# A pairwise-similarity stage: node blocks 15 and 16 away computed from both sides, and fourteen instead of fifteen column blocks added per span

## The reference

```
A = (dist == 1) + eye(N)
nrm = maximum(sqrt(sum(X * X, axis=1)), EPS)
sim = X @ X.T / (nrm[:, None] * nrm[None, :])
m = (A + sim) * 0.5
d = exp(diagonal(m) - logsumexp(m, axis=1))
out = relu(X * d[:, None])
```

## Time and profile before

| | |
|---|---|
| median of three runs | 365.58 us |
| profiled execution, its own time | 365.37 us |
| its span, first to last instruction | 363.6 us |
| mean granted TensorE clock | 0.892 |
| VectorE busy | 302.0 us (83%) |
| TensorE matmul busy | 283.4 us (78%) |
| ScalarE busy | 160.1 us (44%) |
| VectorE's adds, L1099 | 73.0 us in 64 instructions |
| span matmuls, L1394 | 64.7 us in 256 |
| span exponentials, L752 | 60.1 us in 32 |

### The profile page before, as it was taken

The page is one execution under the profiler, slowest core; times in us unless marked ns, Lnnn a source line. Parts: engine busy times, 40 slices in busy tenths (PEclk is TensorE's granted clock), DMA queues, the critical chain, the costliest instruction groups (busy, mean ns, idle before and its releaser), DMA issues.

```text
span 363.6 us, 5779 instructions
## 1 busy us (share of the span) xinstructions
PE 283.4 (78%) x2126; PEld 167.0 (46%) x2126; DVE 302.0 (83%) x422; ACT 160.1 (44%) x251; POOL 102.2 (28%) x107
## 2 busy tenths in 40 slices
PE   7598886118979984599999978758989999965094
PEld 7246754108554431256667623755333333344051
DVE  3899998898367789998688965684999999998764
ACT  1599522200424966500000000397988888994000
POOL 3011069850000098792850005001850000000000
PEclk9899989556999996599999998669999999998569
DMA  3410000000000000000000000344000000000713
GB/s 122 139 46 2 7 6 1 0 0 3 0 2 0 0 0 0 2 0 2 2 2 2 2 1 0 126 107 144 7 0 0 0 0 0 0 3 0 173 58 115
DMA packets 12697, 9.73 MB, mean 27 GB/s; under 512 B 7426, under 2 KB 11010, under 8 KB 12674
## 3 DMA queue, kind: packets, MB, share of 16 engines
q1 hardware_dynamic: 10866, 7.72, 7.4%
q10 hardware_dynamic: 1808, 1.70, 1.6%
HBM read 5.23 MB, written 3.15 MB: 23 GB/s over the span
## 4 chain that ended last, share of the span: by engine, by line
PE 48%; DVE 24%; issue 17%; ACT 4%; ACTq 2%; DMA 2%; DVEq 1%
PE ps L1281 13%; PE ps L1165 11%; PE ps L1178 7%; PE ps L1295 5%; DVE arena L1099 3%; PE ps L1374 2%; PE ps L1197 2%; PE ps L1394 2%; PE ps L1439 2%; DVE arena L365 2%; DVE arena L1015 2%; ACT arena L752 1%; ACTq L344 1%; PE ps L1190 1%; DVE arena L355 1%
## 5 line engine op out<-in xcount | busy, mean ns | idle before, releaser
L1099 DVE TENSOR_TENSOR arena<-arena 128x1024 f32 x64 | 73.0, 1224 | 4.4 <-ACT arena L752 4.4
L1394 PE MATMUL ps<-arena 128*128 (+1 forms) x256 | 64.7, 380 | 6.2 <-ACT arena L752 5.0
L752 ACT ACTIVATE arena<-ps 128x2048 f32<-128x2048 f32 x32 | 60.1, 1877 | 8.5 <-PE ps L1394 6.9
L600 ACT ACTIVATE rstd<-mv,eps 128x2 f32<-128x2 f32 (+1 forms) x5 | 1.5, 296 | 97.5 <-DVE mv L813 97.5
L1394 PEld LDWEIGHTS ps<-arena 128*128 (+1 forms) x256 | 24.4, 97 | 42.1 <-issue 15.8
L1281 PE MATMUL ps<-turns,shift 64*64 64x512 f32 x200 | 36.6, 623 | 4.2 <-DVE turns L1041 4.2
L1165 PE MATMUL ps<-turns,k 128*128 128x512 f32 x80 | 36.5, 618 | 4.2 <-DVE turns L1051 2.1
L1295 PE MATMUL ps<-arena,shift 64*64 64x256 f32 x192 | 34.6, 399 | 6.1 <-DVE arena L1015 6.1
L1041 DVE TENSOR_TENSOR turns<-arena,ps 128x1024 f32<-128x1024 f32 x30 | 35.4, 1216 | 2.4 <-PE ps L1295 2.2
L556 POOL TENSOR_TENSOR arena<-arena 128x2304 f32<-128x2304 f32 x6 | 31.6, 5268 | 16.2 <-PE ps L1295 12.7
L1178 PE MATMUL ps<-arena 64*64 64x240 f32 (+3 forms) x576 | 31.3, 373 | 1.7 <-DVE arena L355 1.7
(11 more groups left out here) (227 smaller groups left out, 503.3 us busy)
## 6 DMA issues: line engine op xcount, KB each, us to landing
scratch_x<-xs SPq DMA_DIRECT2D x4, 256.0 KB
arena<-arena SPq DMA_DIRECT2D x2, 512.0 KB, 3.5
scratch_x<-arena SPq DMA_DIRECT2D x2, 512.0 KB, 3.5
arena<-scratch_x ACTq DMA_DIRECT2D x2, 512.0 KB, 3.7
out<-arena SPq DMA_DIRECT2D x4, 256.0 KB, 2.1
sN<-in_bias_n SPq DMA_DIRECT2D x48, 0.0 KB
xs<-in_x SPq DMA_DIRECT2D x8, 64.0 KB
xs<-in_x ACTq DMA_DIRECT2D x8, 64.0 KB
```

The lines of the kernel that those rows point to most:

```text
L752: act.activation(E[k], ps[:, (k % 2) * 2048:(k % 2 + 1) * 2048], ACT.Exp, scale=0.5 / SPLIT ** 2, accum_out=rowsum[:, bass.ds(i, 1)]).then ...
L1099: dve.tensor_tensor(out=cc, in0=cc, in1=E[k][:, lo * P:hi * P], op=ALU.add).then_inc(sem(name), 1)
L1394: ins = pe.matmul(bank(b0 + q), w, m[:, bass.ds(i * P + 512 * q, 512)], start=(t == 0), stop=(t == 1 and q > 0))
```

## The change

The span is computed as before, 16 blocks wide, row sums included, but only blocks 1 to 14 are added to `colacc`; the far add is 7 blocks (896 columns) instead of 8 (1024). Blocks 15 away therefore lack their mirror image, which is block 17 away of the other row block. The far stage computes it: it has for each row block the blocks 16 and 17 away, 256 columns, in four stages of eight row blocks (`FAR` gives PSUM side and first row block). Stages 1, 2 and 3 all use side 1. On TensorE stages 0 to 2 are issued behind the loop, then the transposes of half 1, then stage 3, then the transposes of half 0. The waits are renumbered: stages 0 and 1 wait for `exp_done` 31 and 32, stage 2 for 34, stage 3 for 35.

```
+        FAR = ((0, 16), (1, 24), (1, 0), (1, 8))
 ScalarE
-            for t in range(2):
+            for t, (side, first) in enumerate(FAR):
                 act.wait_ge(sem("col_near"), NODE_BLOCKS - 2 + t)
                 act.wait_ge(sem("far_done"), t + 1)
-                for i in range(REACH):
-                    c, row = i * P, REACH * (1 - t) + i
-                    ins = act.activation(E[t][:, c:c + P], ps[:, t * 2048 + c:t * 2048 + c + P], ACT.Exp,
+                for i in range(8):
+                    c, row = i * 2 * P, first + i
+                    ins = act.activation(E[t][:, c:c + 2 * P], ps[:, side * 2048 + c:side * 2048 + c + 2 * P], ACT.Exp,
                                          scale=0.5 / SPLIT ** 2, accum_out=row16[:, row:row + 1])
 VectorE
-                for name, lo, hi in (("col_far", 8, REACH), ("col_near", 1, 8)):
+                for name, lo, hi in (("col_far", 8, REACH - 1), ("col_near", 1, 8)):
...
-                dve.wait_ge(sem("exp_done"), NODE_BLOCKS + 2 - h)
+                dve.wait_ge(sem("exp_done"), NODE_BLOCKS + 4 - 2 * h)
 TensorE
-            for t in range(2):
-                pe.wait_ge(sem("exp_done"), NODE_BLOCKS - 1 + t)
-                for i in range(REACH):
-                    ins = half_products(view(ps, t * 2048 + i * P, [(1, P)]), i + REACH * (1 - t), (i + REACH * t) * P, P)
+            def far(t):
+                side, first = FAR[t]
+                pe.wait_ge(sem("exp_done"), NODE_BLOCKS - 1 + t if t < 2 else NODE_BLOCKS + t)
+                for i in range(8):
+                    ins = half_products(view(ps, side * 2048 + i * 2 * P, [(1, 2 * P)]), first + i,
+                                        ((first + i + REACH) % NODE_BLOCKS) * P, 2 * P)
                 ins.then_inc(sem("far_done"), 1)
+
+            for t in range(3):
+                far(t)
             pe.wait_ge(sem("col_far"), NODE_BLOCKS + 1)
             pe.wait_ge(sem("col_near"), NODE_BLOCKS + 1)
             for h in (1, 0):
-                pe.wait_ge(sem("exp_done"), NODE_BLOCKS + 2 - h)
                 if h == 0:
+                    far(3)
                     pe.wait_ge(sem("col_folded"), 1)
+                    pe.wait_ge(sem("exp_done"), NODE_BLOCKS + 4)
```

## The result

The changed kernel takes 369.52 us (median of four runs) against 365.79 us for before: a ratio of 1.0087, 95% interval 1.0056 to 1.0119. Run again beside the experiments it gave 369.95 against 365.57 us, ratio 1.0123 (1.0091 to 1.0155). (The first two medians by themselves divide to 1.0102.) It is slower, by about 1%, and the forecast of 369.6 us holds. The profiled execution has a span of 367.8 us, the very number of the forecast, but not by the very steps; that has to be taken apart.

The account below looks back on a forecast made before the run. Bound: the wait chain through VectorE's adds, transposes, half 1, its DRAM trip and norm. Span 366.2 at full clock, plus 1.6 for half clock gives 367.8, plus 1.77 gives 369.6 us against 365.58; range 367.0 to 371.6.

Parts of the forecast that it names:

- The loop is bound by the round trip between TensorE and ScalarE: Span loop: exponentials keep 4.43 us per two spans, set by one PSUM side's refill; VectorE is merely late.
- Rival 3: Span loop: exponentials really follow VectorE, pitch falls to 2.00 us, 365.5 or 363.9 us, no change; chance 0.07.
- The adds: VectorE: 32 spans lose 128 columns each, 4.3 us, of which 3.3 us is gained; release at 323.5 instead of 326.86.
- Far exponentials: ScalarE's far stage: 256 columns cost 0.36 us each, 2.87 us a stage, four stages 11.5 against 8.0 us.
- Rival 4: Far stage: exponentials near their lower bound, 3.5 us less, 366.1 us; chance 0.09 including anything between it and rival 1.
- rival 5: Matmuls: groups limited by weight loads, so doubling their width would be free; changes nothing in the forecast; no separate chance.
- The order: Far stage: stages 1 to 3 share PSUM side 1, ScalarE waits twice, transposes queue behind; norm 2.6 us late at full clock.
- Behind the far stage: From half 0 to the end: norm follows half 0 on VectorE, then 17.2 us from half 0's load to the end.
- The slack of half 0's branch: Half 0's store and load: 1.97 us to spare before, hiding that much of the delay and no more.
- The clock: TensorE idles 4.3 us before stage 2, so its matmuls run mostly at 1.2 GHz, +1.6 us; forecast chance 0.38.
- rival 1: TensorE's far stage: full clock throughout, span 366.2, 368.0 us; chance 0.27.
- rival 2: TensorE: half clock also catches half 0's transposes, 1.7 us more, span 369.5, 371.3 us; chance 0.17.

Follow-up runs that it names:

- adds_only: Kernel before with only the far adds narrowed to 896 columns, its far stage kept (column sums of blocks 15 away left out): 363.01 us, ratio 0.9928 to before.
- far_only: Changed kernel with far adds 1024 columns wide as before, so only the doubled far stage is new: 370.84 us, ratio 1.0141 to before.
- after: The changed kernel itself, first measurement and trace: 369.52 us, ratio 1.0087 to before.
- after_again: The changed kernel, unedited, profiled and run once more: 369.95 us, ratio 1.0123 to before.
- busy_gap1: Changed kernel plus 13 unneeded matmuls on TensorE in its gap ahead of stage 2: 370.99 us, ratio 1.0138 to before.
- busy_both: Changed kernel plus unneeded TensorE matmuls, 13 ahead of stage 2 and 11 ahead of half 0's transposes: 368.34 us, ratio 1.0077 to before.
- early_wide_adds: Changed kernel with half 1's transposes moved ahead of stages 2 and 3, and far adds 1024 columns again: 366.86 us, ratio 1.0001 to before.
- early_banks: Changed kernel with half 1's transposes ahead of stages 2 and 3, stage 2's matmuls waiting bank by bank for stage 1's exponentials: 364.59 us, ratio 0.9949 to before.

## Why the prediction was right

- **The loop is bound by the round trip between TensorE and ScalarE.** Right: 4.42 us for two spans, last exponential 0.52 us earlier against 0.53 forecast, and adds_only shows the same. Rival 3 falls. The forecast time of the last exponential is the old one less 0.53, not the sum of 4.43 us rounds that the text makes of it: from the 8th exponential to the 32nd are twelve rounds, and they average 4.38 us, before (267.11 to 319.72) as after (265.19 to 317.81).
- **The adds.** Right: released at 71.92, forecast 71.9; VectorE caught up at the 25th span, as forecast, and its 3.3 us bought 0.2 us in the traces and under 1 us by medians (far_only).
- **Far exponentials.** 0.36 us each, as interpolated; stages 0 and 1, with the small exponential, run from 69.63 to TensorE's restart at 75.83 (326.10 - 250.27), forecast 75.9. Rival 4 falls. So does rival 5, in which doubled width would be free: matmuls at full clock follow each other every 0.056 us at 128 columns and every 0.11 us at 256.
- **The order.** Right, and now shown at unchanged work: without the two waits 1.5 us less in the trace and 2.0 by the ratios, with half 1 moved ahead 5 to 6 us less, of which 3.7 to 4.4 us are the order at equal clock. Half 1, which the forecast had at 81.5, is late but not last; half 0 behind it is, as forecast.
- **Behind the far stage.** From half 0 to norm, root, load and end: norm 5.44 us behind half 0's reduction and directly behind half 0, end 20.8 us behind the norm, as in before (112.0 - 91.21). The slack of half 0's branch hid what it was said to hide: its store was issued at 347.04, and its load still went out right behind the root of half 1 (350.49, 350.48).
- **The clock.** Stage 2 at half clock in both traces and in far_only, as forecast, 12 to 16 of its 16 matmuls; rival 1 did not occur. Here the number is better than the step: of the two traces one is the forecast's case (end 116.2, forecast 116.2) and the other is rival 2 (117.5, against 117.9), which came out at the same span only because its front happened to be 1.4 us shorter; that the first trace matches is luck. The chances of 0.38 and 0.17 gave the second slow stretch too little; four traces in this order with a 3.3 us gap ahead of those transposes (after, after_again, far_only, busy_gap1) show it twice.

What decides whether the second stretch falls in an execution stays open; busy_both shows only that in the one trace with the gap filled (0.90 us left) it did not.

## What to carry to other kernels

Work taken off a late engine is worth what the next wait behind it allows: read who waits for that engine's last instruction, and what is queued ahead of that waiter. When work is added behind a loop, its place in the other engines' queues and its buffers can cost more than the work: here the doubled far stage, 3.4 us of added exponentials, cost nothing in one order (early_wide_adds, ratio 1.0001) and 5 us in another (far_only, 1.0141). Compare two traces from a common instruction inside the stage in question, not from their start, before calling a matching total a confirmation.

## What the runs showed of the hardware that was not expected

- The same kernel reaches its first span exponential at 251.65 or 250.83 us (before), 250.27 or 251.65 us (after). The front of the changed kernel alone varies by 1.38 us from one execution to another.
- After 3.27 us of idleness on TensorE the same 16 transposes took 3.65 us at a granted clock of 0.50 in one execution and 1.94 us at 1.00 in another.
- In early_banks the granted clock fell about 1.1 us after TensorE resumed from a gap of 2.05 us, shorter than the 3.27 us after which it stayed at 1.00 in after_again and far_only.
